# Token biases of every second quad, instead of every third, added beforehand by VectorE in blocks 1 and 3

## What is computed

```python
# x: (2, 2048, 512), ctx: (2, 77, 512)
features = layernorm(x)
txt_proj  = einsum('btd,de->bte', ctx, Ws)
feat_proj = einsum('bfd,de->bfe', features, W)
h   = tanh(txt_proj[:, None, :, :] + feat_proj[:, :, None, :] + b)   # rows x 77 tokens x 512
rho = einsum('bftd,d->bft', h, w)                                    # scores
att = softmax(rho masked)
txt_h = att @ ctx
w_s, b_s = tanh(txt_h @ Wcw.T + bcw), tanh(txt_h @ Wcb.T + bcb)
x = x + w_s * features + b_s
# then: xq = fp4(layernorm(x)); g = xq @ fp4(w_gate).T; y = xq @ fp4(w_up).T
#       out = x + fp4(silu(g) * y) @ fp4(w_down).T
```

## Time and profile before

| | |
|---|---|
| median of 3 runs | 1565.66 us (1563.0 to 1566.08) |
| profiled execution, its own time | 1567.96 us |
| span of the profiled execution | 1566.2 us |
| granted TensorE clock, mean | 0.977 of full speed |
| busy share: TensorE, ScalarE, VectorE | 92%, 87%, 75% |

### The profile page before, as it was taken

The page is one execution under the profiler, slowest core; times in us unless marked ns, Lnnn a source line. Parts: engine busy times, 40 slices in busy tenths (PEclk is TensorE's granted clock), DMA queues, the critical chain, the costliest instruction groups (busy, mean ns, idle before and its releaser), DMA issues.

```text
span 1566.2 us, 24368 instructions
## 1 busy us (share of the span) xinstructions
PE 1448.5 (92%) x9752; PEld 644.4 (41%) x9752; DVE 1178.6 (75%) x1952; ACT 1364.5 (87%) x1264; POOL 244.0 (16%) x404
## 2 busy tenths in 40 slices
PE   6978989865999999999999999989999999799998
PEld 3334444411333333343444444434444444455554
DVE  6499999764486666759686776698878777788887
ACT  5999999999999999999999999999999999233331
POOL 1132222210111010111020110111111111112211
PEclk9999999988999999999999999999999999999999
DMA  4133333330011111202111112112211111123332
GB/s 143 41 81 82 84 83 82 83 75 7 8 26 40 39 26 40 40 14 40 40 40 40 40 40 39 26 40 39 40 40 40 39 39 40 40 53 78 78 70 59
DMA packets 180790, 77.91 MB, mean 50 GB/s; under 512 B 163883, under 2 KB 163883, under 8 KB 180677
## 3 DMA queue, kind: packets, MB, share of 16 engines
q1 hardware_dynamic: 179984, 75.00, 21.1%
q10 hardware_dynamic: 693, 1.36, 0.3%
HBM read 27.85 MB, written 8.39 MB: 23 GB/s over the span
## 4 chain that ended last, share of the span: by engine, by line
PE 61%; DVE 18%; ACT 18%; DMA 1%; issue 1%; POOL 0%; SPq 0%; ACTq 0%; DVEq 0%; POOLq 0%
PE rho L749 23%; ACT hring L574 12%; PE dn L839 11%; PE gu0g L827 6%; PE gu0u L827 5%; PE gu1g L827 5%; PE gu1u L827 5%; ACT hring L569 4%; DVE work L946 2%; DVE work L964 1%; DVE work L965 1%; DVE sm L934 1%; ACT featT L574 1%; DVE featT L914 1%; DVE bn L1014 1%
## 5 line engine op out<-in xcount | busy, mean ns | idle before, releaser
L574 ACT ACTIVATE hring<-featT,bias 128x1024 f32<-128x1024 f32 x724 | 765.2, 1145 | 12.4 <-PE rho L749 12.4
L749 PE MATMUL rho<-hring,wslide 128*32 128x512 f32 x3840 | 470.2, 613 | 65.1 <-ACT hring L574 58.5
L749 PEld LDWEIGHTS rho<-hring,wslide 128*32 128x32 f32 x3840 | 105.8, 110 | 338.7 <-issue 196.0
L839 PE MATMUL dn<-wd_room,turned 128*128 128x512 f16 x1023 | 236.2, 383 | 8.7 <-DMA turned<-work 8.7
L569 ACT ACTIVATE hring<-featT 128x4096 f32<-128x4096 f32 x57 | 206.3, 3618 | 0.6 <-DVE featT L914 0.6
L471 POOL TENSOR_SCALAR split_t<-sm 128x88 f32<-128x88 f32 (+2 forms) x91 | 22.4, 246 | 1170.1 <-DVE sm L937 1170.0
L574 ACT ACTIVATE featT<-featT,bias 128x1024 f32<-128x1024 f32 x180 | 192.3, 1154 | 0.7 <-PE rho L749 0.7
L914 DVE TENSOR_SCALAR featT<-featT,bias 128x1024 f32<-128x1024 f32 x256 | 175.5, 749 | 8.5 <-ACT hring L569 6.3
L1213 DVE TENSOR_TENSOR work<-sg,gu1u 128x352 f32<-128x352 f32 x64 | 33.4, 521 | 186.3 <-ACT sg L607 185.9
L839 PEld LDWEIGHTS dn<-wd_room,turned 128*128 128x128 f16 x1023 | 95.7, 99 | 166.8 <-issue 54.9
L827 PE MATMUL gu0g<-wg,turned 128*128 128x352 f16 x768 | 127.5, 316 | 2.4 <-DVE work L1213 2.4
(11 more groups left out here) (192 smaller groups left out, 1618.8 us busy)
## 6 DMA issues: line engine op xcount, KB each, us to landing
xt<-in_x SPq DMA_DIRECT2D x32, 256.0 KB, 2.9
out<-xt SPq DMA_DIRECT2D x32, 256.0 KB, 2.4
work<-in_x SPq DMA_DIRECT2D x10, 512.0 KB, 3.9
xt<-in_x SPq DMA_DIRECT2D x6, 512.0 KB, 3.9
xt<-in_L_ffn_w_gate SPq DMA_DIRECT2D x11, 256.0 KB, 2.7
xt<-in_L_ffn_w_up SPq DMA_DIRECT2D x11, 256.0 KB, 2.7
work<-in_L_ffn_w_down SPq DMA_DIRECT2D x2, 704.0 KB, 4.4
xt<-in_L_ffn_w_down SPq DMA_DIRECT2D x2, 704.0 KB, 4.4
```

What stands on the lines that cost most here:

```text
L574: act.activation(slot[s][:, g, :], featT[:, e, ROW0[k]:ROW0[k] + rows], ACT.Tanh, bias=bias[:, e, base + tok:base + tok + 1]).then_inc(tan ...
L749: last = pe.matmul(rho[SLOTW * g:SLOTW * g + SLOTW, hf * 512:hf * 512 + 512], wslide[:, e, SLOTW - 1 - r:2 * SLOTW - 1 - r], slot[s][:, g, ...
L839: last = pe.matmul(dn[:, :], hqT[:, a, c, :], wd[:, bb, c, :], start=(c == 0 and i == 0), stop=(c == NC - 1 and i == 2))
```

## The change

`SUMS` of block 1 goes from every third quad to every second one: from q = 12, 15, ... 75 (22 quads) to q = 12, 14, ... 72 (31 quads). In block 3 the part from q = 11 on goes from every third (11, 14, ... 74) to every second (11, 13, ... 71), so that it has 33 summed quads in place of 24. Block 2 stays at 18. `AHEAD` of block 1 goes from 4 to 3. As the number of summed quads ahead of block 3 becomes odd (49 in place of 40), the two rooms of block 3 swap their parts.

```diff
-AHEAD = {1: 4, 2: 5, 3: 6}
+AHEAD = {1: 3, 2: 5, 3: 6}
@@
-    SUMS = {1: range(12, QPB, 3), 2: [3, *range(11, QPB, 4)], 3: [2, 5, *range(11, QPB, 3)]}
+    SUMS = {1: range(12, QPB - 4, 2), 2: [3, *range(11, QPB, 4)], 3: [2, 5, *range(11, QPB - 4, 2)]}
```

## The result

The changed kernel takes 1599.95 us (median of 4 runs, 1598.72 to 1603.12), the kernel before beside it 1564.66: the ratio is 1.0229, with a 95% interval of 1.0210 to 1.0248. It is slower by 35.3 us; forecast were 36.4. The profiled execution took 1599.34 us, its span is 1597.2.

The account below looks back on a forecast made before the run. ScalarE was taken to bound block 1, ScalarE and TensorE to be full in block 2, TensorE in block 3. Block 1 + 36.4 us, blocks 2 and 3 0: 1565.66 + 36.4 = 1602 us, range 1588 to 1618.

Parts of the forecast that it names:

- The price of a quad and the place of the gain: ScalarE: plain quad 4.16 us, summed 3.51, 0.65 saved each; a shorter ScalarE can pay in block 1 only, 5.9 us.
- The sum: Block 1, silu (0, 2) to silu (6, 0): ScalarE's work 241.3 us + 44.2 of late sums = 285.5.
- The single waits: Block 1: 22 listed summed quads come late for ScalarE, by 0.33 to 3.63 us each, together 44.2 us.
- The end of block 1: Silu (6, 0) comes near 699, 35.8 us later; one plain quad behind it adds 0.65; block 1 + 36.4 us.
- TensorE: Block 1: its work doesn't grow; it waits for ScalarE 50 us or more, single waits about 1.5 us, or 2.7.
- Rival (c), the clock: Block 1: two waits in each of five tiles lower TensorE's clock, 16.5 us if none hidden: 1618.5; chance 0.08.
- the 1.9 us of small waits: Block 1, kernel before, up to silu (6, 0): rows say 249.7 us, the method 247.8; + 1.9 in the range's high end.
- Rival (a), the gain: Block 1: the lateness is not there, idle VectorE sums in time, ScalarE's 5.9 us come through: 1559.8; chance 0.05.
- the rule of the most-contended engine: Optimise the engine with the highest occupancy first: in block 1 ScalarE, 291.8 of 294 us, so the change gives 5.9 us.
- the single room: Block 1: the sum of quad n can't start before the tanh of n - 2 is read; VectorE's play 1.1 to 1.5 us.
- Blocks 2 and 3: Block 2 changes only its start; block 3's 5.9 us off ScalarE are worth 0, TensorE being full; bounds - 5.9, + 4.5.
- The range: Whole kernel: low - 10.3 if late sums were half as late; high + 1.9, + 4.5, + 3; with part of (c) 1588 to 1618.

Follow-up runs that it names:

- b1_only: Against the kernel before, only block 1 changed: every second quad summed, AHEAD 3; block 3 stays as before. 1600.63 us, ratio 1.0217.
- b1_two_rooms_ahead5: Against the kernel before, block 1 sums every second quad into two rooms in turn, AHEAD 5; block 3 works on other numbers. 1560.14 us, ratio 0.9973.
- b1_picked: Against the kernel before, only block 1 changed: 27 summed quads at uneven distances in place of 22, AHEAD 5. 1557.80 us, ratio 0.9960.
- b1_two_rooms_ahead3: Against the kernel before, block 1 sums every second quad into two rooms in turn, AHEAD 3; block 3 works on other numbers. 1597.78 us, ratio 1.0207.
- b1_ahead4: Against the kernel before, only block 1 changed: every second quad summed, AHEAD stays at 4. 1576.21 us, ratio 1.0067.
- b3_only: Against the kernel before, only block 3 changed: 33 summed quads in place of 24. 1562.27 us, ratio 0.9978.
- b1_odd: Against the kernel before, only block 1 changed: every second quad from q = 13, so even quad numbers are summed, AHEAD 3. 1602.68 us, ratio 1.0239.
- b3_fewer: Against the kernel before, only block 3 changed: 13 summed quads in place of 24. 1566.15 us, ratio 1.0009.

## Why the prediction was right

- **The price of a quad and the place of the gain.** From start to start, as the sum used it, the changed kernel has the same prices: 3.52 us for a summed quad (600.38 to 603.90) and 4.16 for a plain one (603.90 to 608.06). Busy time fell by only 8.6 us over the span in place of the 11.8 that 18 quads at 0.65 make; it is another measure, as two instructions that follow each other without a wait overlap by 0.1 us.
- **The sum.** From silu (0, 2) at 410.04 to silu (6, 0) at 695.73 the changed kernel takes 285.7 us, worked out were 285.5, and the kernel before 249.7. From silu (6, 0) to the drain it takes 0.65 us more (19.53 for 18.88), as the one plain quad there was priced. This is the step that carried the forecast.
- **The single waits.** 22 late sums were listed, 44.2 us together; the profile has 20 of them, 40.3 us, in the listed places. The wait that the profile writes down begins 0.10 us later than the point from which the list counts (3.52 for 3.62), which is 2 us of the difference. With the 0.10 taken off, 17 agree within 0.1. Three don't: 89 (1.98 in place of 1.46), 121 (0.37 in place of 1.37) and 149 (2.12 in place of 2.63); 113 (0.33) starts 0.22 late, which isn't written as a wait, and in the place of 147 (0.33) the wait is put down to a score. In b1_only, with the same block 1, the three waits are 1.47, 1.37 and 2.62. For 121 the cause can be read: ScalarE first waits for a score, and the sum behind it, ready at its own time, is late by as much less.

```profile
548.99 4.27 ACT L574 ACTIVATE hring<-featT,bias 128x1024 f32<-128x1024 f32 x4 [0.87 <-PE rho L749]
...
561.99 3.62 ACT L569 ACTIVATE hring<-featT 128x4096 f32<-128x4096 f32 x1 [0.37 <-DVE featT L914]
```

  This is also why the 1.9 us of small waits that the sum left out do not stand on top of it: the waits for scores before 121, 147 and 149 only took the place of lateness.
- **The end of block 1.** 36.4 us were expected, the profiles say 34.4 (356.2 - 321.8), and 36 to 37 against the 319.6 to 319.9 us which the same block 1 took in the three kernels that change only block 3. The 2 us lie ahead of silu (0, 2), where the instructions are the same: 53.2 us from the drain to it in the kernel before, 51.0 in the changed one. Silu (6, 0) was expected near 699 and starts at 695.7, since the head and these first 50 us of block 1 were 3.8 us shorter in this execution, not since the block lost less. For block 1's part of it the last section gives a cause, for the head there is none.
- **TensorE.** The waits for tanhs grew from 20.7 to 47.4 us, a little under the 50 that were named, the longest 2.9 us:

```profile
PE rho L749 <- ACT hring L569: 23.7, 17, 2.9
PE rho L749 <- ACT hring L574: 23.7, 16, 2.2
```

- **Rival (c), the clock.** The granted clock of block 1 fell from 0.99 to 0.97 (390 to 720 us), so the waits do touch it. TensorE stood 12 times for 2.2 us or more in front of a score. Behind six of these waits the 16 matmuls of the score took 3.2 to 3.6 us, behind the other six the usual 1.92. Two of the waits are equally long, and the length alone doesn't decide it. The two stretches (columns as in the earlier trace rows) have a granted clock of 1.00, the upper level all through, and of 0.72, a mean of both levels:

```profile
452.13 1.92 PE L749 MATMUL rho<-hring,wslide 128*32 128x512 f32 x16 [2.23 <-ACT hring L574]
...
461.89 3.52 PE L749 MATMUL rho<-hring,wslide 128*32 128x512 f32 x16 [2.23 <-ACT hring L574]
...
452.00:456.00 4.00, 3.87 (x30) 1.77 (x31) 2.38 (x4) 2.35 (x3) 0.00 (x0) 1.00 0.01 4
460.00:464.00 4.00, 2.11 (x12) 0.60 (x16) 1.68 (x3) 2.19 (x3) 0.00 (x0) 0.72 0.08 15
```

  The six slow scores are 8.7 us of TensorE, but ScalarE sets the pace there, and the time between the two silus came out 0.2 us over the sum without them. The wait of 0.87 us above is one that did reach ScalarE (the score at 539.82 took 3.27 us), and the late sum behind it took it up. The rival counted ten dips and hid none of them; six came, and between the two silus these runs show no cost of them. A dip elsewhere did cost something (last section).
- **Rival (a), the gain.** It fell on the point named: VectorE does sit idle, 7.56 us in front of the very product, but its order doesn't let it make the sum. In b1_two_rooms_ahead5 and b1_picked it is made real in part: when the sums come in time, the stretch between the two silus is 4.0 and 3.1 us shorter than before. So the rule of the most-contended engine was right about the engine (Perfetto Trace Analysis, section Identifying the Most-Contended Engine, in the Trainium skill); what the rule leaves open is whether the relief arrives in time.
- **The reason given.** The prediction put the single room first, "VectorE has only 1.1 to 1.5 us of play", and AHEAD second. The sum was right since it went through the calls one by one, but the weight was not: with AHEAD 3 a second room left ScalarE's waits for sums at 39.6 us in place of 40.8, and the stretch between the two silus at 285.5 us in place of 285.1 (b1_two_rooms_ahead3; of the 1.8 us between their blocks 1, 1.6 are a wait at the start, last section), and one step of AHEAD alone gives 24 of the 35 us back (b1_ahead4). The room is shown to cost something at AHEAD 5 (12 us). At AHEAD 4 VectorE waits longer for it than at 3 (24.4 us for 13.5), but no run with two rooms says what that costs. The pieces of 5.9 to 7.2 us count since VectorE passes the call too late, not since the room is taken.
- **Blocks 2 and 3.** Block 2 kept its 323.6 us in all profiles. Block 3, taken at 0 between - 5.9 and + 4.5, was + 0.1 us.
- **The range.** Its lower end, 1588, is not the sum of its terms: 1602 - 10.3 is 1592. The measured 1599.95 lies above both.

## What to carry to other kernels

Work prepared ahead by a second engine pays only if it is ready when the bottleneck engine asks: go through the calls of both in-order programs with their start-to-start times, and look for the item that is wanted directly behind the event which its own producer waits for. How far ahead the producer may look and how many buffers it has are two limits of their own: here a second buffer showed nothing while the reach was 3, and was worth 12 us when it was 5. A regular pattern (every second, every third) laid over an uneven schedule meets such places by chance; a choice that was checked place by place gained here, with four items fewer. How long the producer stands still says little by itself; what comes late behind it counts.

## What was not expected

The stretches whose instructions are the same in all these kernels don't always take the same time. The head ran from 358.3 to 361.3 us, the tail from 230.5 to 233.7, and block 1 with the old sums 321.8 in one kernel and 319.6 to 319.9 in three others.

The spread of block 1 lies between its first drain and silu (0, 2): 53.2 us in the kernel before, 51.0 to 51.3 in the three others; behind that the four agree to 0.04 us up to silu (6, 0). The granted clock differs there, 0.84 in the kernel before and 0.91 in b3_only:

```profile
360.00:415.00 55.00, 42.19 (x284) 15.01 (x280) 28.77 (x72) 52.95 (x56) 3.81 (x8) 0.84 0.03 6
```

```profile
360.00:415.00 55.00, 42.66 (x298) 16.00 (x299) 28.92 (x73) 54.81 (x56) 3.83 (x8) 0.91 0.03 6
```

Most of the 2 us can be read off. Behind the drain TensorE transposes the scores in two groups (L814) with a quad's scoring between. In the kernel before, the granted clock is 0.60 from 364 to 368 us; the scoring takes 2.99 us in place of 1.92 and the second group 1.68 in place of 1.12. It ends later by that, and ScalarE has to stand for the softmax step that needs it:

```profile
366.01 1.68 PE L814 MATMUL tr<-gat,stage 128*128 128x77 f32 x8
...
368.82 0.46 ACT L582 ACTIVATE stage<-stage 128x308 f32<-128x308 f32 x1 [1.56 <-DVE stage L1137]
```

In b3_only the clock is 1.00 there and ScalarE doesn't stand:

```profile
363.45 1.12 PE L814 MATMUL tr<-gat,stage 128*128 128x77 f32 x8
```

The four kernels with such a wait of 1.6 us (before, b1_only, b1_odd, b1_ahead4) are those in which the second group took 1.58 to 1.78 us; in the nine others it took 1.11 or 1.12. Here a lowered clock did lengthen a block. Why the clock fell there in some profiles and not in others was not found out. Neither was the spread of the head, which doesn't go with it (360.8 us in b3_fewer, without the wait), nor that of the tail. The profile of the kernel before is of a longish execution, 1567.96 us against medians of 1564.66 to 1565.69, so part of the differences to it may be this execution's.

Why the runs with more sums in block 3 come out ahead (2.5 and 3.4 us by the ratios) was not found out either; one profile of each doesn't tell whether the dip is rarer in them. A difference of 3 us between two of these kernels is therefore no proof of a change in the stretch that was edited; the length of that stretch, between two instructions inside it, is the better witness.
